# Pairs counted two in a number, and the attention layer's masks and words taken from other places

## The chip, the cores and the metric

The kernel runs on one core of one Trainium2 chip. The metric is the device time of one execution in microseconds (us), lower being better. Before the change it is 4636.71 us, the median of three runs (4636.35 to 4637.34).

## The reference

A graph of N = 3125 nodes with 256 features each and E = 50,000 edges, sorted by destination, goes through four graph layers, with a residual and a layer normalization around each:

```python
edge_index = jnp.stack([src, dst])
x = _layernorm(x + _L0_gnn_ref(x, edge_index, W, b))            # degree-normalized sum over edges, then @ W
x = _layernorm(x + _L1_gnn_ref(x, src, dst, ...))               # attention over each node's edges, 8 heads of 32
x = _layernorm(x + _L2_gnn_ref(x, edge_index, ...))             # attention, then three mean-aggregation layers
x = _layernorm(x + _L3_gnn_ref(x, weight, edge_weight1, src, dst, edge_type_16))   # 16 relations
```

Of the first layer, what the change concerns is how often each pair (destination, source) occurs and how many edges begin and end at each node. Of the second:

```python
e = leaky_relu(el[src] + er[dst], 0.2);  m = segment_max(e, dst);  e = exp(e - m[dst])
a = e / segment_sum(e, dst)[dst];        out = segment_sum(feat[src] * a[:, :, None], dst)
```

## The kernel before

Nodes lie in T = 25 tiles of 128. Edges lie in S = 416 slots of 128, each slot belonging to one tile of destinations; `words_i` has one number for every four slots, which says where among them one tile ends and the next begins. Each function of the kernel is a block: the five engines run their own programs in it, order them by semaphores, and meet at its end.

**Counting pairs** (`count_pairs`, L479 to L634, called once). For each slot, VectorE (DVE) writes two one-hot matrices in bfloat16. `hot_d` (L536) is 128 edges x 128 destinations. `hot_s` is 128 edges x 3125 sources, in two instructions (L538: 1600 columns, L540: 1525), because a comparison number beyond 2048 isn't exact in float16. TensorE (PE) multiplies the two into `counts`, seven PSUM banks of up to 512 columns (`product`, L560), which collect over all slots of a tile. A 3126th column of ones gives the edges per destination. Where a tile ends inside a group of four slots, PE closes the banks (L557), ScalarE (ACT) copies each to `rows` (L621), and SyncE stores the 128 x 3200 numbers to `pairs_d` (L630); PE's next product into a bank waits for its copy. `marked` and `hist` (L525, L527, L576) count the edges per source in the same loop, once for four slots. `hot_d` and `hot_s` have four buffers, handed back by `used`. PE alone reads `words_i` (`load_word`, L81), by a load into a register of its sequencer.

**The attention layer** (`attend`, L1323 to L1694) walks the slots in 13 parts of 32. GpSimd (POOL) gathers a slot's 128 rows of `feat_d` with one indirect DMA (L1377) into `got`, which holds two parts. When a part has arrived, PE turns its scores (L1561). DVE and PE find the maximum per destination (`maximum`, from L1437 to L1488). PE deals the next scores out into `spreads` (`deal`, L1539). DVE then writes, for every four slots, the masks `hot` (L1498: `iota` compared with `dloc`) and the weighed rows (L1502), eight times in a part. PE multiplies them into `sums` (L1604) behind a matmul that restores the carried sums (L1599), and reads the part's eight words just ahead of it (`total`).

Of the kernel before, what the change touches and what calls it, by code (L numbers as in the profile page):

```python
# [478 lines left out]
def count_pairs(nc, k, pairs_d, links_d):  # L479
# [7 lines left out]
    with ExitStack() as c:  # L487
# [23 lines left out]
        @block.gpsimd  # L511
        def _(pool):
            pool.iota(places[:], [[1, HALF]], base=0, channel_multiplier=0,
                      allow_small_or_imprecise_dtypes=True).then_inc(ready, 1)
            pool.memset(zero[:], 0.0).then_inc(ready, 1)
            pool.memset(hot_s[:, :, N:N + 1], 1.0).then_inc(ready, 1)
            pool.memset(rows[:, :, N:NP], 0.0).then_inc(ready, 1)

        @block.vector
        def _(dve):  # L520
            dve.tensor_scalar(upper[:], k.src[:], float(-HALF), None, ALU.add).then_inc(ready, 1)
            dve.wait_ge(ready, 5)
# [7 lines left out]
            with dve.Fori(0, S // 8) as i:  # L530
                for u in range(8):
                    j = i * 8 + u
                    if u % 4 == 0:
                        marks(2 * i + u // 4, u // 4)
                    dve.wait_ge(used, j + 1)
                    dve.tensor_scalar(hot_d[:, u % 4, :], k.iota_b[:], cols(k.dloc, j, 1), None,  # L536
                                      ALU.is_equal).then_inc(made, 1)
                    dve.tensor_scalar(hot_s[:, u % 4, 0:HALF], places[:], cols(k.src, j, 1), None,  # L538
                                      ALU.is_equal).then_inc(made, 1)
                    dve.tensor_scalar(hot_s[:, u % 4, HALF:N], places[:, 0:N - HALF], cols(upper, j, 1), None,  # L540
                                      ALU.is_equal).then_inc(made, 1)
            dve.wait_ge(final, 1)
            dve.tensor_copy(k.deg_src[:], hist[:, 0:T])

        @block.tensor
        def _(pe):
            pe.sem_inc(used, 4)
            pe.sem_inc(tallied, 2)
            pe.wait_ge(ready, 5)

# [12 lines left out]
            def multiply(u, j):  # L563
                pe.wait_ge(made, j * 3 + 3)
# [14 lines left out]
            def four(i, b):  # L579
                tally(i, b)  # L580
                word = load_word(pe, k, i)
                with pe.If((word & 15) == 0):
                    for u in range(4):
                        multiply(u, i * 4 + u)
                with pe.If((word & 15) != 0):

                    for u in range(4):
                        with pe.If(turn_here(word, u) == 0):
                            multiply(u, i * 4 + u)
                        with pe.If(turn_here(word, u) != 0):  # L590
                            t = tile_before(word, u)
                            for b in range(BANKS):
                                end(b).then_inc(full, 1)
                            pe.wait_ge(made, (i * 4 + u) * 3 + 3)
                            for b in range(BANKS):

                                pe.wait_ge(copied, t * COPIES + COPIES + (b + 1 if b < BANKS - 1 else COPIES))
                                last = product(u, b, True)
                            last.then_inc(used, 1)
# [4 lines left out]
            pe.matmul(hist[:, 0:T], zero[0:EP, 0:P], zero[0:EP, 0:T], start=False, stop=True).then_inc(final, 1)  # L604
            for b in range(BANKS):
                end(b).then_inc(full, 1)

        @block.scalar
        def _(act):
            act.sem_inc(copied, COPIES)  # L610

            def copy(t, b):
                if reused(t):
                    act.wait_ge(stored[b], (t - b) * 8)
                act.sem_inc(k.passed, 1)
                for n in range(BANKS):
                    act.wait_ge(full, t * BANKS + n + 1)
                    act.sem_inc(k.passed, 1)
                    if n == BANKS - 1:
                        act.copy(cols(k.deg_dst, t, 1), counts[:, n, width[n]:width[n] + 1]).then_inc(copied, 1)  # L620
                    act.copy(rows[:, b, n * 512:n * 512 + width[n]], counts[:, n, 0:width[n]]).then_inc(copied, 1)  # L621
            over_tiles_after_two(act, copy)

        @block.sync
        def _(sp):
            sp.dma_start(links_d.rearrange("d (g q) p -> q d g p", q=SQ), k.links[:]).then_inc(linked, 16)

            def store(t, b):
                sp.wait_ge(copied, t * COPIES + 2 * COPIES)
                sp.dma_start(pairs_d[bass.ds(t * P, P), :], rows[:, b, :]).then_inc(stored[b], 16)  # L630
# [692 lines left out]
def attend(nc, k, table, links_d, er, acc, den):  # L1323
# [6 lines left out]
    with ExitStack() as c:  # L1330
# [62 lines left out]
        def _(dve):  # L1393
# [97 lines left out]
            def weigh(n):  # L1491
                b = n % 2
                dve.wait_ge(weights, 2 * n + 1)
                for g in range(NG):
                    if n >= 1:
                        dve.wait_ge(multiplied, (n - 1) * NG + g + 1)
                    j = n * CS + 4 * g
                    dve.tensor_tensor(hot[:, 4 * g:4 * g + 4, :], k.iota[:].unsqueeze(1).broadcast_to([P, 4, P]),  # L1498
                                      k.dloc[:, j:j + 4].unsqueeze(2).broadcast_to([P, 4, P]), ALU.is_equal).then_inc(made, 1)
# [3 lines left out]
                                      ALU.mult).then_inc(weighed, 1)  # L1503

            step(dve.memset(penx[:], -BIG))
            dve.sem_inc(cleared, 1)
# [25 lines left out]
        def _(pe):  # L1532
# [61 lines left out]

            def total(n, b, more):
                words = [load_word(pe, k, n * NG + g) for g in range(NG)]
                pe.wait_ge(resumed, n + 1)
# [35 lines left out]
            pe.wait_ge(er_kept, 1)  # L1633
            deal(0)
            pe.wait_ge(seamed, 1)
# [344 lines left out]
def graph_layers(nc, x, src, dst, edge_type_16, edge_weight1, L0_gnn_W, L0_gnn_b, L1_gnn_W_lin, L1_gnn_b_lin,  # L1980
# [12 lines left out]
    with ExitStack() as c:  # L1993
# [9 lines left out]
        k.zero = sb("zero", [P, T])  # L2003
        k.unordered = sb("unordered", [1, 1], I32)
        k.words_i = sb("words_i", [1, S // 4], I32)
        k.parts_i = sb("parts_i", [1, NC], I32)
# [10 lines left out]
        with ExitStack() as l:  # L2017
# [5 lines left out]
            order_edges(nc, k, [src, dst, edge_type_16, edge_weight1.rearrange("e a -> (e a)").bitcast(I32)], dst)  # L2023
            fill_slots(nc, k)
            count_pairs(nc, k, pairs_d, links_d)

# [226 lines left out]
```

## Time and profile before

| | us |
|---|---|
| median of three runs | 4636.71 |
| the profiled execution, whole | 4640.11 |
| its span in the profile | 4638.3 |
| PE, DVE, POOL, ACT busy | 3766.8, 1928.5, 1310.2, 578.0 |
| counting pairs, first mark to the next block | 83.0 to 756.2 |
| gathers of the attention layer, first to last | 1243.2 to 1813.9 |

The profile gives for each engine its busy time and what it waited for. A matmul in it is a weight load (PEld) and a product (PE). A granted clock of 1.00 is 2.4 GHz and 0.50 is 1.2 GHz. Names such as `c_`, `a_` and `t_` before a tile are those of the function: counting, attention, first layer.

### The profile page before, as it was taken

How to read it: one execution, taken by the hardware profiler on the slowest of the kernel's cores; microseconds unless marked ns; L12 is line 12 of the kernel's file. 1: busy time of each engine (PE TensorE's matmuls, PEld its weight loads, DVE VectorE, ACT ScalarE, POOL GpSimd, SP SyncE). 2: the span in 40 equal slices, each digit the busy share in tenths (PEclk: the TensorE clock that was granted, in tenths of full speed). 3: DMA queues.
4: the chain of work that ended last, by engine and by line, in shares of the span. 5: the costliest groups of instructions: out<-in, count | busy, mean ns of one | idle time of the engine just before them, and what ended most of it. 6: DMA issues, size and time to landing. Idle time of an engine off the chain costs nothing. (4 is left out here: it accounts for less than half of the span.)

```text
span 4638.3 us, 49117 instructions
## 1 busy us (share of the span) xinstructions
PE 3766.8 (81%) x14814; PEld 2235.0 (48%) x14871; DVE 1928.5 (42%) x4570; ACT 578.0 (12%) x1119; POOL 1310.2 (28%) x923
## 2 busy tenths in 40 slices
PE   3999988996646666379999979999999689965665
PEld 1444434564445454256666645655655434434444
DVE  6998884012467777633232201211122411132223
ACT  0001112222101001012222200000000012200000
POOL 1000000000277775027777600000000000047776
PEclk9999999998767777689999989999999899987787
DMA  1011125763244442011221143443433134433334
GB/s 49 14 42 58 83 99 189 234 217 129 93 120 124 116 126 64 12 74 61 76 75 62 61 160 117 136 136 116 138 134 116 49 131 145 145 119 105 104 105 120
DMA packets 240236, 493.51 MB, mean 106 GB/s; under 512 B 22617, under 2 KB 137853, under 8 KB 231885
## 3 DMA queue, kind: packets, MB, share of 16 engines
q1 hardware_dynamic: 199693, 380.62, 23.8%
q0 software_dynamic: 40448, 111.66, 8.6%
q8 instruction: 54, 0.88, 0.1%
q14 instruction: 41, 0.34, 0.0%
HBM read 347.63 MB, written 145.38 MB: 106 GB/s over the span
## 5 line engine op out<-in xcount | busy, mean ns | idle before, releaser
L1257 POOL DMA_INDIRECT e7got<-rel_d,rel_i x416 | 394.9, 949 | 1551.3 <-POOLq L2138 1424.8
L1377 POOL DMA_INDIRECT a_got<-feat_d,src_i x416 | 445.2, 1070 | 1287.0 <-POOLq L1703 1160.6
L560 PE MATMUL c_counts<-c_hot_s,c_hot_d 128*128 128x512 bf16 (+1 forms) x2857 | 603.0, 357 | 49.6 <-ACT c_rows L621 18.2
L946 PE MATMUL s_aggs<-s_blk,h 128*128 128x512 f32 (+1 forms) x1400 | 549.6, 549 | 17.9 <-DMA s_blk<-turned_d 17.9
L1293 PE MATMUL e7sums<-e7got,e7hot 128*128 128x256 f32 x832 | 289.7, 508 | 194.1 <-DMA e7got<-rel_d,rel_i 164.9
L560 PEld LDWEIGHTS c_counts<-c_hot_s,c_hot_d 128*128 128x128 bf16 x2912 | 258.7, 98 | 366.6 <-ACT c_rows L621 66.1
L946 PEld LDWEIGHTS s_aggs<-s_blk,h 128*128 128x128 f32 x1400 | 264.2, 191 | 268.6 <-issue 176.2
L2179 PE MATMUL q_prods<-w,q_xt 128*128 128x512 f32 x800 | 352.8, 599 | 13.4 <-ACT q_xt L2197 13.4
L1038 DVE TENSOR_SCALAR s_zs<-s_prods,col 128x256 f32<-128x256 f32 x75 | 36.3, 484 | 751.7 <-PE s_prods L972 751.7
L1293 PEld LDWEIGHTS e7sums<-e7got,e7hot 128*128 128x128 f32 x832 | 204.5, 256 | 276.4 <-issue 238.0
L1109 POOL TENSOR_SCALAR g_absent<-g_pairs 128x3200 bf16<-128x3200 f32 x25 | 274.8, 10992 | 169.4 <-DMA g_pairs<-pairs_d 169.3
L1156 PE MATMUL g_sums<-value,g_turned 128*128 128x257 f32 x1250 | 299.1, 383 | 8.6 <-ACT g_turned L1220 8.6
L1134 PE MATMUL g_scores<-key_t,g_q 128*128 128x512 f32 (+1 forms) x700 | 278.3, 554 | 27.4 <-DMA g_q<-query_d 20.3
L811 PE MATMUL t_aggs<-t_blk,r 128*128 128x512 f32 (+1 forms) x700 | 299.5, 550 | 0.0
L946 PE MATMUL s_aggs<-s_blk,spare 128*128 128x512 f32 (+1 forms) x700 | 273.8, 547 | 0.0
L1265 DVE TENSOR_SCALAR e7hot<-iota,dloc,weight 128x128 f32<-128x128 f32 x416 | 115.8, 364 | 356.7 <-PE e7sums L1293 348.2
L538 DVE TENSOR_SCALAR c_hot_s<-c_places,src 128x1600 bf16<-128x1600 f16 x416 | 261.9, 630 | 0.0
L540 DVE TENSOR_SCALAR c_hot_s<-c_places,c_upper 128x1525 bf16<-128x1525 f16 x416 | 255.8, 615 | 0.0
L2179 PEld LDWEIGHTS q_prods<-w,q_xt 128*128 128x128 f32 x800 | 151.0, 191 | 200.6 <-issue 199.9
L1156 PEld LDWEIGHTS g_sums<-value,g_turned 128*128 128x128 f32 x1250 | 226.4, 191 | 43.1 <-issue 7.6
L1604 PE MATMUL a_sums<-a_got,a_hot 128*128 128x264 f32 x832 | 234.3, 444 | 0.2
L1134 PEld LDWEIGHTS g_scores<-key_t,g_q 128*128 128x128 f32 x700 | 130.0, 192 | 176.8 <-issue 142.0
(365 smaller groups left out, 4056.9 us busy)
## 6 DMA issues: line engine op xcount, KB each, us to landing
s_blk<-turned_d SPq DMA_DIRECT2D x60, 1280.0 KB, 5.7
rel_d<-q_rows SPq DMA_DIRECT2D x25, 2048.0 KB, 7.5
s_blk<-turned_d SPq DMA_DIRECT2D x45, 960.0 KB, 4.9
pairs_d<-c_rows SPq DMA_DIRECT2D x25, 1600.0 KB, 5.2
g_pairs<-pairs_d SPq DMA_DIRECT2D x25, 1600.0 KB, 6.6
t_blk<-pairs_d SPq DMA_DIRECT2D x20, 1280.0 KB, 7.1
turned_d<-t_line SPq DMA_DIRECT2D x20, 1280.0 KB, 9.7
t_blk<-pairs_d SPq DMA_DIRECT2D x15, 960.0 KB, 6.1
```

The lines of the kernel that those rows point to most:

```text
L538: dve.tensor_scalar(hot_s[:, u % 4, 0:HALF], places[:], cols(k.src, j, 1), None, ALU.is_equal).then_inc(made, 1)
L540: dve.tensor_scalar(hot_s[:, u % 4, HALF:N], places[:, 0:N - HALF], cols(upper, j, 1), None, ALU.is_equal).then_inc(made, 1)
L560: return pe.matmul(counts[:, b, 0:taken[b]], hot_d[:, u, :], hot_s[:, u, b * 512:b * 512 + taken[b]], start=first, stop=False)
L811: last = pe.matmul(aggs[:, n % 2, half, 0:w], r[:, a, half * P:(half + 1) * P], blk[:, q % RINGS, a % GA, 0:w], start=a == 0, stop=a == T - 1)
L946: last = pe.matmul(aggs[:, idx % 2, half, 0:w], feats[l][:, a, half * P:(half + 1) * P], blk[:, q % RINGS, a % GA, 0:w], start=a == 0, sto ...
L1109: pool.tensor_scalar(absent[:, b, :], pairs[:, b, :], 0.0, -BIG, ALU.is_equal, ALU.mult).then_inc(flagged, 1)
L1134: last = pe.matmul(scores[:, n % BUFS, 0:width[n]], q[:, b, a, :], key_t[:, a, n * 512:n * 512 + width[n]], start=a == 0, stop=a == 1)
L1156: last = pe.matmul(sums[:, b, 0:D + 1], turned[:, g % BUFS, a % 4, :], value[:, a, :], start=a == 0, stop=a == T - 1)
L1257: pool.indirect_dma_start(got[:, j % U, :], None, table, bass.IndirectOffsetOnAxis(ap=index[:, j:j + 1], axis=0)).then_inc(arrived[j % U / ...
L1293: return pe.matmul(sums[:, 0:D], hot[:, u, :], got[:, u, :], start=False, stop=False)
L1377: pool.indirect_dma_start(got[:, n % 2, s, :], None, table, bass.IndirectOffsetOnAxis(ap=k.src_i[:, j:j + 1], axis=0)).then_inc(arrived[n ...
L2179: last = pe.matmul(prods[:, o % 4, :], xt[:, b, a, :], w[:, a, 2 * o:2 * o + 2, :].rearrange("p r n -> p (r n)"), start=a == 0, stop=a == 1)
```

## The change

**Counting pairs.** A new block, `count_packed`, does the work of `count_pairs` with one column for two sources: source s and source s + 1563 share column s. A low source adds 1 to its column and a high one 4096, so a number in PSUM holds two counts of up to 4095. `hot_s` is one instruction of 1563 columns, which compares and multiplies by two per-partition numbers; a slot's product takes four banks (512, 512, 512 and 28 columns) in place of seven. `hot_d` and `hot_s` have eight buffers. When a tile closes, ACT copies the banks to `whole` as integers; DVE, two groups later, takes the low 12 bits and the high ones (`take_apart`); ACT copies both to `rows`, as float. To know that a tile has closed, DVE now reads the word of the group two back, in every group of four slots. The old block stays behind the new one, and each engine skips it unless `heavy`, computed at the new block's end, says that some node has more than 4095 edges.

```diff
+def count_packed(nc, k, pairs_d, links_d):
+    HALF = (N + 1) // 2
+    W = HALF + 1
+    LOOK = 2
+    RING = 4 * LOOK
...
+            step(dve.tensor_scalar(high[:], k.src[:], float(HALF), None, ALU.is_ge))
+            step(dve.scalar_tensor_tensor(column[:], high[:], float(-HALF), k.src[:], ALU.mult, ALU.add))
+            step(dve.tensor_scalar(value[:], high[:], 4095.0, 1.0, ALU.mult, ALU.add))
...
+            def take_apart(t):
+                dve.wait_ge(copied, t * COPIES + 2 * COPIES)
+                dve.wait_ge(spread_out, t * 2 + 2)
+                dve.tensor_single_scalar(apart[:, 0, :], whole[:], 4095, ALU.bitwise_and).then_inc(parted, 1)
+                dve.tensor_single_scalar(apart[:, 1, :], whole[:], 12, ALU.arith_shift_right).then_inc(parted, 1)
+
+            def closings(group):
+                word = load_word(dve, k, group)
+                with dve.If((word & 15) != 0):
+                    for u in range(4):
+                        with dve.If(turn_here(word, u) != 0):
+                            take_apart(tile_before(word, u))
...
-                    dve.tensor_scalar(hot_s[:, u % 4, 0:HALF], places[:], cols(k.src, j, 1), None,
-                                      ALU.is_equal).then_inc(made, 1)
-                    dve.tensor_scalar(hot_s[:, u % 4, HALF:N], places[:, 0:N - HALF], cols(upper, j, 1), None,
-                                      ALU.is_equal).then_inc(made, 1)
+                    dve.tensor_scalar(hot_s[:, u, 0:HALF], places[:, 0:HALF], cols(column, j, 1), cols(value, j, 1),
+                                      ALU.is_equal, ALU.mult).then_inc(made, 1)
...
+                    act.copy(whole[:, n * 512:n * 512 + here], counts[:, n, 0:here]).then_inc(copied, 1)
...
+                for half in range(2):
+                    act.wait_ge(parted, t * 2 + half + 3)
+                    act.copy(rows[:, b, half * HALF:(half + 1) * HALF], apart[:, half, :]).then_inc(spread_out, 1)
```

In the counting loop, DVE's program for one slot was (the ISA and ALU rows are its sequencer's)

```order
L535 REGISTER_ALU
L536 ISA
L536 TENSOR_SCALAR c_hot_d<-iota_b,dloc 128x128
L538 REGISTER_ALU
L538 TENSOR_SCALAR c_hot_s<-c_places,src 128x1600
L540 REGISTER_ALU
L540 TENSOR_SCALAR c_hot_s<-c_places,c_upper 128x1525
```

and is now

```order
L726 REGISTER_ALU
L727 ISA
L727 TENSOR_SCALAR u_hot_d<-iota_b,dloc 128x128
L728 ISA
L728 TENSOR_SCALAR u_hot_s<-u_places,u_column,u_value 128x1563
```

Ahead of each group of four slots its program now has (L81 is the word, L714 the test whether a tile closes in the group, L716 the same for one slot, L705 and L707 the waits of `take_apart`)

```order
L81 TENSOR_LOAD words_i
L81 ISA x2
L714 REGISTER_ALU
L714 COMPARE_AND_BRANCH
L716 REGISTER_ALU
L716 COMPARE_AND_BRANCH
L705 ISA
L707 ISA
L709 TENSOR_SCALAR u_apart<-u_whole 128x1563
L710 TENSOR_SCALAR u_apart<-u_whole 128x1563
```

A slot went from three instructions to two, and a load with a test came in front of each group.

**The attention layer.** The masks' `iota` is copied once into PSUM, to the free columns of `spreads`, and L1498 reads it there; since `deal` writes the same bank, DVE waits before a part's masks until the deal issued just before them has ended. PE's eight words of a part are loaded at its start, ahead of `maximum`.

```diff
                 dve.wait_ge(weights, 2 * n + 1)
+                dve.wait_ge(dealt, min(n + 3, NC + 1))
...
-                    dve.tensor_tensor(hot[:, 4 * g:4 * g + 4, :], k.iota[:].unsqueeze(1).broadcast_to([P, 4, P]),
+                    dve.tensor_tensor(hot[:, 4 * g:4 * g + 4, :], spreads[:, 256:256 + P].unsqueeze(1).broadcast_to([P, 4, P]),
...
             def chunk(n, b, more):
+                words = [load_word(pe, k, n * NG + g) for g in range(NG)]
                 maximum(n, b, more)
-                total(n, b, more)
+                total(n, b, more, words)
```

PE's program around the end of a part's maxima was

```order
L1552 MATMUL a_expand<-a_er,a_pick 128x24 x8
L1539 ISA
L1539 MATMUL a_spreads<-tile_hot,a_er_rows 128x32 x8
L81 ISA
L81 TENSOR_LOAD words_i
L81 ISA x3
```

with seven more such loads before `L1599 MATMUL a_sums<-a_carry,ident`; now the deal is followed directly by the restoring matmul:

```order
L1764 MATMUL a_expand<-a_er,a_pick 128x24 x8
L1751 ISA
L1751 MATMUL a_spreads<-tile_hot,a_er_rows 128x32 x8
L1810 MATMUL a_sums<-a_carry,ident 128x264
```

The eight loads stand at the loop's head instead, ahead of the part's first `a_expand` and of the turned lines (`a_line`) that DVE's maxima wait for.

## Rows read from the trace of the kernel before

**Rows 1.** The profile's page: busy us (share of the span) xinstructions

```profile
PE 3766.8 (81%) x14814; PEld 2235.0 (48%) x14871; DVE 1928.5 (42%) x4570; ACT 578.0 (12%) x1119; POOL 1310.2 (28%) x923
```

**Rows 2.** Waits between 60 and 800 us: total us, times, longest

```profile
DVE c_hot_d L536 <- PE c_counts L560: 53.6, 53, 2.2
```

**Rows 3.** Timeline of the counting, one group: start, us, engine, instruction

```profile
401.06 0.68 DVE L525 TENSOR_TENSOR c_marked<-iota_b,slo 125x512 bf16<-125x512 bf16 x1
...
401.83 0.24 DVE L536 TENSOR_SCALAR c_hot_d<-iota_b,dloc 128x128 bf16<-128x128 bf16 x1
401.99 0.62 DVE L538 TENSOR_SCALAR c_hot_s<-c_places,src 128x1600 bf16<-128x1600 f16 x1
402.54 0.61 DVE L540 TENSOR_SCALAR c_hot_s<-c_places,c_upper 128x1525 bf16<-128x1525 f16 x1
403.07 0.24 DVE L536 TENSOR_SCALAR c_hot_d<-iota_b,dloc 128x128 bf16<-128x128 bf16 x1
...
406.77 0.68 DVE L525 TENSOR_TENSOR c_marked<-iota_b,slo 125x512 bf16<-125x512 bf16 x1
```

**Rows 4.** Stretches: us, busy of PE PEld DVE ACT POOL, clock, DMA, GB/s

```profile
90.00:150.00 60.00, 56.84 (x331) 26.75 (x334) 59.71 (x147) 0.00 (x0) 0.00 (x0) 1.00 0.00 1
1500.00:1600.00 100.00, 60.09 (x305) 47.15 (x303) 73.08 (x122) 8.21 (x17) 77.76 (x74) 0.73 0.45 130
```

**Rows 5.** Timeline of PE's weight loads after a tile's end

```profile
207.61 0.15 PEld L560 LDWEIGHTS c_counts<-c_hot_s,c_hot_d 128*128 128x128 bf16 x1 [0.28 <-issue]
208.04 0.15 PEld L560 LDWEIGHTS c_counts<-c_hot_s,c_hot_d 128*128 128x128 bf16 x1 [0.28 <-issue]
...
210.35 0.18 PEld L576 LDWEIGHTS c_hist<-c_marked 125*128 125x128 bf16 x4
...
215.79 0.18 PEld L576 LDWEIGHTS c_hist<-c_marked 125*128 125x128 bf16 x4
```

**Rows 6.** DVE's timeline: one per-partition number, then two

```profile
759.45 6.66 DVE L875 TENSOR_SCALAR r<-X,col 128x256 f32<-128x256 f32 x25
...
4628.58 1.38 DVE L1908 TENSOR_SCALAR acc<-acc,mv,rstd 128x256 f32<-128x256 f32 x4
```

**Rows 7.** DVE's groups, busy us, mean ns: integers; an odd number of columns

```profile
L200 DVE TENSOR_SCALAR p_bits<-p_sn 125x400 int32<-125x400 int32 x1 | 0.4, 369 | 3.4 <-DMA p_nxt<-in_dst 3.4
L238 DVE TENSOR_SCALAR p_cmpj<-p_ioj,p_ends 25x417 f32<-25x417 f32 x1 | 0.4, 425 | 0.0
```

**Rows 8.** A part's word loads, 1510 to 1531 us: ns min/median/max, first to last

```profile
L81 PEldq TENSOR_LOAD <-words_i x8: 297/298/309, 1524.8 to 1530.1; - x8
```

**Rows 9.** An ACT group over SBUF: busy us, mean ns

```profile
L1213 ACT ACTIVATE g_probs<-g_probs,g_top 128x3200 f32<-128x3200 f32 x25 | 74.1, 2964 | 26.4 <-DVEq L1188 26.4
```

**Rows 10.** SyncE's timeline, the first load of the block after the counting

```profile
756.23 6.84 SPq L778 DMA_DIRECT2D t_blk<-pairs_d  x5
```

**Rows 11.** DVE's register load ahead of a block that it skips

```profile
L349 DVEq TENSOR_LOAD <-unordered x1: 546/546/546, 38.9 to 38.9; - x1
```

**Rows 12.** The gathers, and DVE's first scan of a part: ns, first and last start

```profile
L1377 POOL DMA_INDIRECT a_got<-feat_d,src_i x416: 942/946/1823, 1243.2 to 1813.9; - x139
...
L1437 DVE TENSOR_TENSOR_SCAN a_turned<-a_penx,a_turned x13: 2282/2283/2283, 1288.6 to 1819.8; 32x1024 f32<-32x1024 bf16 x13
```

**Rows 13.** Waits between 1155 and 1890 us

```profile
DVE a_turned L1437 <- PE a_turned L1561: 108.5, 13, 24.2
```

**Rows 14.** Timeline of the attention layer: the deal, the masks, the gathers

```profile
1524.66 3.62 PE L1539 MATMUL a_spreads<-tile_hot,a_er_rows 25*128 x16
...
1527.26 0.69 DVE L1498 TENSOR_TENSOR a_hot<-iota,dloc 128x512 f32<-128x512 f32 x1 [0.22 <-DVE a_carry L1488]
...
1529.00 0.68 DVE L1498 TENSOR_TENSOR a_hot<-iota,dloc 128x512 f32<-128x512 f32 x1
1529.08 1.43 POOL L1377 DMA_INDIRECT a_got<-feat_d,src_i  x1 [0.30 <-issue]
1529.60 1.21 DVE L1502 TENSOR_TENSOR a_got<-a_got,a_peaks 128x1024 f32<-128x1024 f32 x1
```

**Rows 15.** DVE's groups: one input in PSUM, both in SBUF

```profile
L1041 DVE TENSOR_TENSOR s_zs<-s_zs,be 128x256 f32<-128x256 f32 x75 | 31.9, 425 | 2.6
L1039 DVE TENSOR_TENSOR s_zs<-s_zs,s_prods 128x256 f32<-128x256 f32 x75 | 31.6, 421 | 2.6
```

More of the change, by code:

```diff
@@ new lines, in _, with copy @@
+        @block.scalar
+        def _(act):
+            heavy = act.value_load(k.heavy[:], min_val=0, max_val=1)
+            with act.If(heavy != 0):
+                act.sem_inc(copied, COPIES)
+                def copy(t, b):
+                    if reused(t):
+                        act.wait_ge(stored[b], (t - b) * 8)
+                    act.sem_inc(k.passed, 1)
+                    for n in range(BANKS):
+                        act.wait_ge(full, t * BANKS + n + 1)
+                        act.sem_inc(k.passed, 1)
+                        if n == BANKS - 1:
+                            act.copy(cols(k.deg_dst, t, 1), counts[:, n, width[n]:width[n] + 1]).then_inc(copied, 1)
+                        act.copy(rows[:, b, n * 512:n * 512 + width[n]], counts[:, n, 0:width[n]]).then_inc(copied, 1)
+                over_tiles_after_two(act, copy)
@@ new lines, in _, with store @@
+        @block.sync
+        def _(sp):
+            heavy = sp.value_load(k.heavy[:], min_val=0, max_val=1)
+            with sp.If(heavy != 0):
+                sp.dma_start(links_d.rearrange("d (g q) p -> q d g p", q=SQ), k.links[:]).then_inc(linked, 16)
+                def store(t, b):
+                    sp.wait_ge(copied, t * COPIES + 2 * COPIES)
+                    sp.dma_start(pairs_d[bass.ds(t * P, P), :], rows[:, b, :]).then_inc(stored[b], 16)
+                over_tiles(sp, store)
+                sp.wait_ge(linked, 16)
+                sp.wait_ge(stored[0], 16 * (T // 2 + 1))
+                sp.wait_ge(stored[1], 16 * (T // 2))
@@ new lines, in count_packed, with _ @@
+def count_packed(nc, k, pairs_d, links_d):
+    HALF = (N + 1) // 2
+    W = HALF + 1
+    BANKS = -(-W // 512)
+    COPIES = BANKS + 1
+    LOOK = 2
+    RING = 4 * LOOK
+    with ExitStack() as c:
+        c.enter_context(nc.cleanup_on_exit())
+        sb = lambda n, s, d=F32: c.enter_context(nc.sbuf_tensor("u_" + n, s, d))
+        sem = lambda n: nc.alloc_semaphore("u_" + n)
+        places = sb("places", [P, HALF + 1], F16)
+        high, column, value = sb("high", [P, S]), sb("column", [P, S]), sb("value", [P, S])
+        hot_d = sb("hot_d", [P, RING, P], BF16)
+        hot_s = sb("hot_s", [P, RING, W], BF16)
+        zero = sb("zero", [P, 512], BF16)
+        whole = sb("whole", [P, HALF], I32)
+        apart = sb("apart", [P, 2, HALF], I32)
+        rows = sb("rows", [P, 2, NP])
+        largest, flag = sb("largest", [P, 1]), sb("flag", [1, 1])
+        marked = sb("marked", [EP, 2, 4, P + T], BF16)
+        hist = c.enter_context(nc.psum_tensor("u_hist", [P, 512], F32))
+        counts = c.enter_context(nc.psum_tensor("u_counts", [P, BANKS, 512], F32))
+        (ready, made, used, hot, tallied, final, full, copied, parted, spread_out, linked, vstep) = (sem(n) for n in (
+            "ready", "made", "used", "hot", "tallied", "final", "full", "copied", "parted", "spread_out", "linked", "vstep"))
+        reduced, laid = sem("reduced"), sem("laid")
+        stored = [sem(f"stored{b}") for b in range(2)]
+        taken = [min(512, W - b * 512) for b in range(BANKS)]
+        block = c.enter_context(nc.Block())
+        @block.gpsimd
+        def _(pool):
+            pool.iota(places[:], [[1, HALF + 1]], base=0, channel_multiplier=0,
@@ L563, in multiply @@
             def multiply(u, j):
[L564 removed]
+                pe.wait_ge(made, j * 2 + 2)
                 for b in range(BANKS):
```

169 lines of the change are left out of this document (139 added, 30 removed).

## The prediction

> **What bounds the kernel now.** I read the page first: PE is busy for most of the span, DVE for under half [rows 1]. Such shares mix stages, so I took the two stages of the change apart, by stretches, waits and timelines.
>
> In the counting, DVE is busy 59.71 of 60 us before the first tile closes, and PE 56.84 [rows 4]. The timeline shows why: a group of four slots takes DVE 5.71 us, mark to mark, 0.77 for the marks and 1.24 for each slot, which is 0.16 (`hot_d`), 0.55 and 0.53 (`hot_s`) from start to start [rows 3]. PE, where it is behind and has not to wait, does a group in 5.44 us [rows 5]. So DVE sets the pace and PE is close behind. DVE's own waits for PE, 53.6 us, come where tiles close and four buffers don't bridge the copies [rows 2].
>
> In the attention layer the waits name the other end. DVE stands 108.5 us for a part's turned scores, 24.2 of it for the first part [rows 13], and these wait for the gathers. A part takes (1819.8 - 1288.6) / 12 = 44.3 us [rows 12]; DVE waits (108.5 - 24.2) / 12 = 7.0 of it, so its own chain is 37.3. POOL's gathers set the pace: one every 1.375 us ((1813.9 - 1243.2) / 415), though one takes 0.946 [rows 12] and 0.30 to issue [rows 14].
>
> **Counting: the masks.** The two `hot_s` instructions become one of 1563 columns. 1600 columns cost 0.55 us and 1525 cost 0.53 [rows 3]; 75 columns for 0.02 us fits four a cycle at 0.96 GHz, also for the odd 1525, and leaves 0.13 us fixed. So 1563 columns are 0.54 us. The second per-partition number costs extra: with one, (6.66 - 0.35) / 24 = 0.263 us from start to start, with two (1.38 - 0.41) / 3 = 0.323, both for 256 float columns [rows 6]. I add 0.06: 0.60 for `hot_s`, 0.76 for a slot, 0.77 + 4 x 0.76 = 3.81 for a group, 396 us for 104 groups. No row shows two per-partition numbers in bfloat16. The bounds are four columns a cycle and one: 0.60 and 1563 / 0.96 + 0.19 = 1.82 us. I take the first, since in floats the two-number form keeps the pace of the one-number form but for the 0.06.
>
> **Counting: taking apart.** 25 tiles bring two integer instructions each. 400 integers took 0.369 us and an odd 417 floats 0.425 [rows 7], less than 417 / 0.96 = 0.434: two a cycle. 1563 / 1.92 + 0.13 = 0.94 us, 50 of them 47 us; at one a cycle it would be 88.
>
> **Counting: words and tests on DVE.** 104 loads and tests. On PE's sequencer a load takes 0.30 us and one follows another after 0.76 [rows 8]; with the test about 0.85. If DVE's sequencer is far enough ahead of its engine, this costs nothing; if not at all, 88 us. In front of a group the queued `hot_s` covers 0.6, and eight buffers let DVE's sequencer run ahead. I take 0.1 each, 10 us.
>
> **Counting: what is late next.** A group of PE's has 12 full matmuls fewer. One is 0.213 us at 2.4 GHz, so 5.44 - 12 x 0.213 = 2.88, under DVE's 3.81; PE waits for DVE throughout. At a closing, PE's four banks come back behind ACT's copies at 0.5 us steps, some 2 us, less than the 3 us of four more slots made. ACT adds two copies of 1563 numbers, 1.45 us each by its 2.96 us for 3200 [rows 9]; with the banks about 5 us of the 9 that even the shortest tile lasts. DVE's `take_apart` waits for copies made two groups before. I allow 20 us for closings in which one waits for the other, against 53.6 now. The loop becomes 396 + 47 + 10 + 20 = 473 us. It was 741.6 - 83.0 = 658.6, that is 104 x 5.71 = 594 and the waits. Gain 185.
>
> **Around the loop.** From DVE's last mask to the next block's first load it was 741.6 to 756.2 [rows 10]. Now PE is less far behind (3 us), three banks fewer are copied (1 us), but 0.94 + 2 x 1.45 us of taking apart come before the last store: no change. The old block is skipped: one register load of 0.55 us [rows 11], a jump over long code and one more meeting of the engines. The trace shows no long jump; 1 to 6 us, I take 3.
>
> **Attention: masks from PSUM.** A gather that starts under a mask (1529.08, mask from 1529.00) takes 1.43 us in place of 0.95, while the weighing (L1502), which has one input in PSUM, lengthens none [rows 14]. A mask and a weighing together last 1.73 us, exactly gather plus issue, so the two lock together, seven or eight times in a part: 7.5 x 0.48 = 3.6 us. That fits the 32 x (1.375 - 1.246) = 4.1 by which a part's gathers are over their undisturbed pace. So the gathers would allow 40.7 us for a part. The read from PSUM itself costs nothing by the one pair that compares it: 421 ns with an input in PSUM, 425 without [rows 15].
>
> Two rules of the Trainium skill speak against this edit. The page "VectorE: DVE Perf Modes", section "The TRN2 errata", gives an instruction with a PSUM source 62 cycles more than one with SBUF sources. By that, as an estimate, 104 masks would lose 7 us, and the time be 4424; the rows just named disagree with it. The page "SBUF — State Buffer", section "Who interferes with whom", says that a `tensor_tensor` with both inputs in SBUF contends only with GpSimd's reads, and infers that it doesn't stall the generation of descriptors. By that a gather would not be longer under a mask and the edit would gain nothing (4455); the 1.43 us row contradicts it here.
>
> **Attention: the wait and the words.** The masks now wait for `deal`. It ends at 1524.66 + 3.62 = 1528.28, and the first mask starts at 1527.26 [rows 14]: 1.0 us later, and behind it stand all weighings, PE's products and the next part's scores. The eight words take 8 x 0.76 = 6.1 us of PE's sequencer [rows 8]. Until now they delayed PE behind the deal, where DVE wasn't waiting. At the head they run while PE's engine still works off the last part's products, but what isn't finished delays the turned lines that DVE's maxima need: 0 to 6.1 us, I take 1.5, because some 4.5 us of queued products stand in front. DVE's chain becomes 37.3 + 1.0 + 1.5 = 39.8 us, just under the gathers' 40.7. So a part gains up to 3.6 us, 12 parts 43; as the two ends are so close I take 38.
>
> **Sum.** The profiled execution took 4640.1 us (span 4638.3 and 1.8 around it): 4640.1 - 185 + 3 - 38 = 4420. It was 3.4 us above the median of the three runs, so I predict 4417.
>
> **Rivals.**
> 1. *The attention layer gives nothing.* The words at the head delay DVE by their whole 6.1 us: 37.3 + 1.0 + 6.1 = 44.4, the part's period of now. For it: DVE waits for these very lines soon after PE's last products. Against it: those products are queued ahead. 4417 + 38 = 4455. Chance 0.16.
> 2. *DVE pays for control and integers in full.* 78 us more for the words, 41 for one integer a cycle; 10 more at the arms: 4546. Against it: rows 7, and the deeper buffers. 0.10 for this or most of it.
> 3. *TensorE drops to 1.2 GHz and becomes the bound.* In the counting the clock is 1.00 with PE busy 95%, in the attention layer 0.73 with 60% [rows 4]; the new counting would be near 75%. After a closing's wait, loads follow at 0.43 us [rows 5], which is 1.2 GHz. Held there, a group costs PE 12 x 0.43 + 0.35 = 5.5 us, 104 of them 573, with closings 615, not 473: 4559. Against it: it would then be busy without gaps, and that is where these rows show the full clock. 0.06.
> 4. *The double mask doesn't run four columns a cycle.* At two, a slot is 1.17 us and the loop 654: 4598, chance 0.03. At one, a slot is 1.98 us, a group 8.7, the loop 904 + 47 + 20 = 971: 4417 + 498 = 4915, slower than before. This is the case on the other side; it decides once `hot_s` costs more than about 1.15 us, where the loop passes 658.6 + 35. It has no row against it in the same types, only the float rows. 0.04.
>
> **Chances.** The forecast has 0.61, with 4380 to 4450 for itself: the loop between 443 and 493 us, the attention layer between 43 and 25. Range 4375 to 4500: it holds rival 1 and half of rival 2, and leaves out the other half, rival 3 and rival 4. A change under 0.2% can't be told from none here. Faster 0.94 (all but rival 4 at one column, and mixes of its half pace with exposed words), same 0.01, slower 0.05.
>
> **What would show it.** Right: `hot_s` at about 0.68 us in the groups and 0.60 from start to start; `apart` at about 1.0 us; groups 3.8 to 4.0 us apart before the first tile closes; the loop over by 560 us. Gathers at 0.95 us under the masks, and first scans 41 us apart. Wrong: `hot_s` over 1 us; gaps of 0.5 us and more in front of the marks with DVE's sequencer loading a word; PE's matmuls at 0.43 us through the stage; DVE waiting for `turned` not at all in the attention layer, with 44 us between scans.

## The result, and the profile after

The changed kernel takes 4389.53 us (median of four runs, 4388.77 to 4392.23), the one before 4636.53 beside it (4634.40 to 4637.34). The ratio is 0.9469, with the 95% interval 0.9453 to 0.9485: faster by 247 us. The forecast was 4417, with 4375 to 4500 as range.

The page of the changed kernel answers to [rows 1]: span 4387.5 us, PE 273 us less busy, DVE 154.

```profile
PE 3493.4 (80%) x13533; PEld 2105.8 (48%) x13546; DVE 1774.5 (40%) x4212; ACT 612.8 (14%) x1094; POOL 1269.4 (29%) x923
```

**The counting.** A stretch before the first tile closes (us, busy of PE, PEld, DVE, ACT, POOL, clock, DMA, GB/s) answers to [rows 4]. DVE has no gap, and PE is now 81% busy in place of 95%, still at the full clock.

```profile
90.00:140.00 50.00, 40.42 (x274) 19.40 (x273) 50.00 (x132) 0.00 (x0) 0.00 (x0) 1.00 0.00 0
```

DVE's timeline (start, us, engine, instruction) shows a group, answering to [rows 3], and a closing behind the next one:

```profile
300.14 0.69 DVE L699 TENSOR_TENSOR u_marked<-iota_b,slo 125x512 bf16<-125x512 bf16 x1
...
300.91 0.25 DVE L727 TENSOR_SCALAR u_hot_d<-iota_b,dloc 128x128 bf16<-128x128 bf16 x1
301.08 0.69 DVE L728 TENSOR_SCALAR u_hot_s<-u_places,u_column,u_value 128x1563 bf16<-128x1563 f16 x1
301.67 0.25 DVE L727 TENSOR_SCALAR u_hot_d<-iota_b,dloc 128x128 bf16<-128x128 bf16 x1
...
303.95 0.69 DVE L699 TENSOR_TENSOR u_marked<-iota_b,slo 125x512 bf16<-125x512 bf16 x1
...
307.77 0.97 DVE L709 TENSOR_SCALAR u_apart<-u_whole 128x1563 int32<-128x1563 int32 x1
308.66 0.97 DVE L710 TENSOR_SCALAR u_apart<-u_whole 128x1563 int32<-128x1563 int32 x1
309.54 0.69 DVE L699 TENSOR_TENSOR u_marked<-iota_b,slo 125x512 bf16<-125x512 bf16 x1
```

Mark to mark is 303.95 - 300.14 = 3.81 us; a slot is 0.76 (300.91 to 301.67), of which `hot_s` has 0.60 from start to start. A closing (the two integer instructions that follow where a tile ended) costs 309.54 - 307.77 = 1.77. The marks at 303.95 start with no gap, though DVE's program has a word loaded and tested ahead of them. Over the whole loop the answer for DVE's line of `hot_s` (ns min/median/max, first and last start) and that of the integers, with what DVE waited for there, are

```profile
L728 DVE TENSOR_SCALAR u_hot_s<-u_places,u_column,u_value x416: 673/689/703, 84.4 to 520.7; 128x1563 bf16<-128x1563 f16 x139
```

```profile
L709 DVE TENSOR_SCALAR u_apart<-u_whole x25: 957/970/980, 167.4 to 527.1; 128x1563 int32<-128x1563 int32 x25
its engine sat idle before it (us, times) until:
  ACT u_whole L824: 4.0, 1
  issue: 0.2, 1
```

The 4.0 us are those of the last tile, behind the loop. Inside it DVE waits for nobody; the wait of [rows 2] is gone, and PE waits for DVE instead (total us, times, longest):

```profile
PE u_counts L761 <- DVE u_hot_d L727: 42.3, 50, 1.9
```

The loop, first mark to where DVE's last `hot_s` gives way to the next instruction, is 521.3 - 83.5 = 437.8 us against 658.6: 221 us less. What follows is longer. DVE's and SyncE's timeline from the loop's end to the next block, for [rows 10]:

```profile
520.71 0.69 DVE L728 TENSOR_SCALAR u_hot_s<-u_places,u_column,u_value 128x1563 bf16<-128x1563 f16 x1
...
527.15 0.97 DVE L709 TENSOR_SCALAR u_apart<-u_whole 128x1563 int32<-128x1563 int32 x1 [3.99 <-ACT u_whole L824]
...
530.22 0.14 DVE L744 CAST heavy<-u_flag 1x1 int32<-1x1 f32 x1
542.21 7.07 SPq L988 DMA_DIRECT2D t_blk<-pairs_d  x5
```

That is 20.9 us where it was 14.6. The next block starts 756.23 - 542.21 = 214.0 us earlier.

**The attention layer.** Its first gather starts 213.9 us earlier. The gathers and DVE's first scan of each part, for [rows 12]:

```profile
L1587 POOL DMA_INDIRECT a_got<-feat_d,src_i x416: 942/946/1851, 1029.3 to 1559.4; - x139
```

```profile
L1647 DVE TENSOR_TENSOR_SCAN a_turned<-a_penx,a_turned x13: 2282/2283/2283, 1074.4 to 1568.8; 32x1024 f32<-32x1024 bf16 x13
```

A part takes (1568.8 - 1074.4) / 12 = 41.2 us in place of 44.3, and the gathers take 530.1 us from first to last in place of 570.7. The last scan is 37 us nearer to the first gather (539.5 in place of 576.6), the last mask 34 (572.9 in place of 606.5). The masks of before and of after, in the same columns:

```profile
L1498 DVE TENSOR_TENSOR a_hot<-iota,dloc x104: 679/683/693, 1305.8 to 1849.7; 128x512 f32<-128x512 f32 x104
```

```profile
L1709 DVE TENSOR_TENSOR a_hot<-a_spreads,dloc x104: 680/681/692, 1093.0 to 1602.2; 128x512 f32<-128x512 f32 x104
```

DVE's waits there, for [rows 13]:

```profile
DVE a_turned L1647 <- PE a_turned L1773: 41.5, 9, 24.3
DVE a_hot L1709 <- PE a_spreads L1751: 15.1, 12, 1.6
DVE a_lines L1658 <- PE a_small L1782: 13.1, 9, 5.9
```

Besides the old wait for the turned scores there are two new ones: the masks for the deal, 1.3 us a part, and the lines, for which PE is late because of its words. The timeline of a part's masks answers to [rows 14]:

```profile
1298.99 0.69 DVE L1709 TENSOR_TENSOR a_hot<-a_spreads,dloc 128x512 f32<-128x512 f32 x1 [1.34 <-PE a_spreads L1751]
...
1300.11 0.94 POOL L1587 DMA_INDIRECT a_got<-feat_d,src_i  x1 [0.30 <-issue]
1300.72 0.68 DVE L1709 TENSOR_TENSOR a_hot<-a_spreads,dloc 128x512 f32<-128x512 f32 x1
1301.32 1.21 DVE L1713 TENSOR_TENSOR a_got<-a_got,a_peaks 128x1024 f32<-128x1024 f32 x1
1301.35 0.94 POOL L1587 DMA_INDIRECT a_got<-feat_d,src_i  x1 [0.30 <-issue]
...
1302.45 0.68 DVE L1709 TENSOR_TENSOR a_hot<-a_spreads,dloc 128x512 f32<-128x512 f32 x1
1302.60 0.95 POOL L1587 DMA_INDIRECT a_got<-feat_d,src_i  x1 [0.31 <-issue]
```

The gather of 1302.60 starts 0.15 us into a mask and takes 0.95 us. (The one of 1300.11 is no test: it is there before its mask, and such gathers weren't lengthened in the kernel before either.) Counted over both traces: in the kernel before, 95 gathers start while a mask runs; those that start 0.07 us into it take 1.43 us, those 0.45 us into it 1.06. In the 12 during which a mask starts, none takes over 0.95. In the changed kernel 56 start while a mask runs and 71 have one start during them, and none takes over 0.96.

214.0 and 33.6 us make 247.6; the spans differ by 250.8. The other 3 lie in the layers behind, which the change doesn't touch.

### The profile page after: what moved, and what is told of

The parts are those of the page before. It is cut to its first block and busy times, and to the rows that moved or that the text cites. A ratio compares the mean times of both kernels' runs of the same rounds, so it can differ in the third digit from the quotient of the medians.

```text
span 4387.5 us, 46641 instructions
## 1 busy us (share of the span) xinstructions
PE 3493.4 (80%) x13533; PEld 2105.8 (48%) x13546; DVE 1774.5 (40%) x4212; ACT 612.8 (14%) x1094; POOL 1269.4 (29%) x923
## 5 line engine op out<-in xcount | busy, mean ns | idle before, releaser
L1587 POOL DMA_INDIRECT a_got<-feat_d,src_i x416 | 404.6, 973 | 1072.6 <-POOLq L1916 946.3
L761 PE MATMUL u_counts<-u_hot_s,u_hot_d 128*128 128x512 bf16 (+1 forms) x1653 | 328.6, 341 | 90.5 <-DVE u_hot_d L727 42.3
L728 DVE TENSOR_SCALAR u_hot_s<-u_places,u_column,u_value 128x1563 bf16<-128x1563 f16 x416 | 286.6, 689 | 0.0
L761 PEld LDWEIGHTS u_counts<-u_hot_s,u_hot_d 128*128 128x128 bf16 x1664 | 136.6, 99 | 256.9 <-DVE u_hot_d L727 53.1
L1815 PEld LDWEIGHTS a_sums<-a_got,a_hot 128*128 128x128 f32 x832 | 177.2, 221 | 64.1 <-issue 28.7
```

The source lines that it names most:

```text
L728: dve.tensor_scalar(hot_s[:, u, 0:HALF], places[:, 0:HALF], cols(column, j, 1), cols(value, j, 1), ALU.is_equal, ALU.mult).then_inc(made, 1)
L761: return pe.matmul(counts[:, b, 0:taken[b]], hot_d[:, u, :], hot_s[:, u, b * 512:b * 512 + taken[b]], start=first, stop=False)
L1587: pool.indirect_dma_start(got[:, n % 2, s, :], None, table, bass.IndirectOffsetOnAxis(ap=k.src_i[:, j:j + 1], axis=0)).then_inc(arrived[n ...
L1815: ins = pe.matmul(sums[:, 0:W], hot[:, 4 * g + u, :], got[:, b, 4 * g + u, :], start=False, stop=False)
```

## The experiments

Two questions were open: how much each part of the change gives, and why the counting loop was 35 us shorter than I had worked out. The first four kernels ran on one chip with the kernel before (4637.52 us, seven runs).

**c_only.** `count_packed` as changed, `attend` as before.

> The counting part of the change alone, the attention layer as before. Theory (the two parts are independent; the counting gave 214 us of the 247 and the attention layer 37, as the two profiles read side by side): 4636.5 - 214 = about 4423 us, and the gathers 1.375 us apart again. Rival (the counting gave the 182 us that the prediction gave it, and the rest comes from the two parts together): about 4455 us.

Measured: 4425.52 us (4422.67 to 4427.52), ratio 0.9543 [0.9527, 0.9559]. So the counting gives 212 us; the trace of the changed kernel had said 214. Its gathers (busy us, mean ns, then idle time) are still long, 1069 ns in the mean:

```profile
L1587 POOL DMA_INDIRECT a_got<-feat_d,src_i x416 | 444.5, 1069 | 1073.0 <-POOLq L1913 946.6 <-issue 125.8 <-PE a_sums L1814 0.6
```

**a_only.** `attend` as changed, counting as before.

> The attention layer's part alone, the counting as before. Theory: 4636.5 - 37 = about 4600 us, a part's first scans 41.2 us apart. Rival (the attention layer gains only behind the shorter counting): 4636 us.

Measured: 4608.26 us (4607.73 to 4608.45), 0.9937 [0.9920, 0.9953]: 29 us less, 8 short of what I expected. After c_only's 4425.5, the attention part is worth 36. Inside the layer both do the same: 529.8 us of gathers (mean 972 ns), 572.9 to the last mask, 33.6 less than before. The difference of 7 isn't in the layer. Between the profiled executions it is 3: with the new counting the span is 34.7 us shorter (32.1 of it in the layer), with the old one 31.9 (33.6 in the layer).

**a_masks_old.** The changed kernel with the masks reading `iota` in SBUF and no wait for the deal; the words stay at the head.

```diff
-                dve.wait_ge(dealt, min(n + 3, NC + 1))
...
-                    dve.tensor_tensor(hot[...], spreads[:, 256:256 + P].unsqueeze(1).broadcast_to([P, 4, P]),
+                    dve.tensor_tensor(hot[...], k.iota[:].unsqueeze(1).broadcast_to([P, 4, P]),
```

> The changed kernel with the masks read from SBUF again and without their wait for the deal; the words stay at the part's head. Theory: the gathers take 1.43 us under a mask again, first scans 44.3 us apart, 4389.5 + 37 = about 4427 us. Rival (the words bring at least half of the gain): 4408 us or less.

Measured: 4430.20 us (4428.65 to 4431.02), 0.9553 [0.9537, 0.9569]; gathers 1031.8 to 1600.0, the old pace. The words alone gain nothing; against c_only they cost some 5 us, and they cost them at the end: from the last scan to the last mask it is 35.2 us here and 29.4 in c_only.

**a_words_old.** The changed kernel with the words behind the deal.

```diff
-                words = [load_word(pe, k, n * NG + g) for g in range(NG)]
                 maximum(n, b, more)
-                total(n, b, more, words)
+                total(n, b, more)        # which loads the words itself, at its start
```

> The changed kernel with TensorE's eight words loaded where they were, behind the deal; the masks still read PSUM and wait for the deal. Theory (the masks alone bring the attention layer's gain, and the words at the head only delay the turned lines, by 16.9 us in ten parts): DVE waits for the lines no more, first scans 40.9 us apart in place of 41.2, about 4386 us, no slower than 4390. Rival (the words' new place is what lets TensorE follow, so without it each part is 2.6 us longer): about 4420 us.

Measured: 4380.11 us (4379.57 to 4382.99), 0.9445 [0.9429, 0.9460], 9 us under the changed kernel. That one was measured in another series, and the two intervals just touch, so the 9 us rest on the traces below and on the last run of this section as well. So the masks from PSUM gave 45 us against c_only, and the words at the head took back 9. The gathers of this kernel,

```profile
L1587 POOL DMA_INDIRECT a_got<-feat_d,src_i x416 | 404.3, 972 | 1074.7 <-POOLq L1916 948.2 <-issue 124.9 <-PE a_sums L1816 1.5
```

are those of the changed one (mean 973), from the first to the last 529.8 us against 530.1. So the middle parts gain nothing from either place of the words. By the traces the 9 us lie where no gather is left to issue. PE's timeline in the last part, changed kernel first:

```profile
1567.62 1.04 PE L1773 MATMUL a_turned<-ident,a_got 128*32 128x128 f32 x8
...
1573.16 0.28 PE L1805 MATMUL a_sums<-zero_b 128*128 128x264 bf16 x1
1578.11 0.37 PE L1782 MATMUL a_small<-ident,a_line 32*8 32x32 f32 x4 [4.68 <-issue]
```

```profile
1565.19 1.03 PE L1773 MATMUL a_turned<-ident,a_got 128*32 128x128 f32 x8 [0.41 <-DMA a_got<-feat_d,src_i]
...
1571.55 0.27 PE L1782 MATMUL a_small<-ident,a_line 32*8 32x32 f32 x4 [0.55 <-DVEq L1652]
```

The last gathers start at 1559.4 and 1561.3. With the words behind the deal PE waits for that gather's rows and turns them 3.9 us after it was issued; with the words ahead it is still busy with products that its late start had pushed back, and turns them 8.3 us after. Then PE's engine stands 4.68 us with nothing but the sequencer's loads between two matmuls, and DVE stands 3.8 us for the lines. The last scan starts 9.4 us after the last gather in one kernel and 5.1 in the other: 4.3 + 3.8 = 8.1 us, of the 9.4 between the medians.

**c_ring4 and c_words3.** Four buffers for `hot_d` and `hot_s` in place of eight; and each word of DVE loaded three times. The next four kernels ran on a chip where the kernel before took 4936.52 us. Their gathers take 754 to 767 us from first to last, against 530, though each instruction still takes 0.97 in the mean; so only what lies inside the counting loop is compared with the runs above. DVE's instructions there have the same length (`hot_s` 685 ns).

```diff
-    RING = 4 * LOOK
+    RING = 4          # and every buffer index u taken mod 4
```
```diff
                 word = load_word(dve, k, group)
+                word = load_word(dve, k, group)
+                word = load_word(dve, k, group)
```

> The changed kernel with four buffers for the counting's masks in place of eight. Theory (eight buffers are what took DVE's waits for TensorE, 53.6 us, away and let its sequencer hide the words): DVE waits at each of 24 closings some 1 to 2 us and in some groups for the word: 4389.5 + 40 = about 4430. Rival (with four banks in place of seven TensorE is so far ahead that four buffers would do): 4395 or less.

Measured: 4836.56 us, 0.9796 [0.9750, 0.9843]. The loop is 84 us longer, twice what I expected:

```profile
L728 DVE TENSOR_SCALAR u_hot_s<-u_places,u_column,u_value x416: 679/685/699, 84.6 to 605.4; 128x1563 bf16<-128x1563 f16 x139
```

Its waits of DVE in the loop:

```profile
DVE u_apart L709 <- issue: 40.5, 23, 2.4
DVE u_hot_d L727 <- PE u_counts L761: 31.0, 48, 2.0
DVE u_marked L699 <- issue: 4.5, 9, 0.7
```

31 us are the old wait for PE at closings, which eight buffers cover. 40.5 us stand in front of the 23 closings in the loop with nothing named but issue: there, as I read it, DVE's sequencer had stood with its engine for a buffer, and so was not ahead when the closing's tests came. The 31 us are to be held against the 53.6 of [rows 2], with four buffers and seven banks.

> The changed kernel with DVE loading each word three times. Two more loads are 1.5 us of its sequencer per group, 2.4 us with the first, against 3.8 us of its engine. Theory (the sequencer runs ahead of the engine by the depth of its queue, and a load costs nothing while it does): the queue covers one load but not three, the groups grow by some 0 to 1 us: 4390 to 4490, middle 4420. Rival (loads never show while the sequencer's sum is under the engine's 3.8 us): 4390, no change. Second rival (a load that is not covered by chance costs all of its 0.76): 4389.5 + 104 x 1.5 = 4546.

Measured: 4806.55 us, 0.9740 [0.9694, 0.9785]. The loop is 576.5 - 83.5 = 493.0 us between first and last `hot_s`, 56.7 longer (inside what I expected), for 208 loads more: 0.27 us each. Its waits in the loop:

```profile
DVE u_apart L709 <- issue: 31.9, 23, 2.3
DVE u_marked L699 <- issue: 16.5, 34, 0.8
```

Even with three loads only 34 marks of 103 stand, half a microsecond each; most of the cost is at the closings, as in c_ring4. There too the marks hardly stand (4.5 us), so a group's single load and test are nearly hidden with four buffers as well. What four buffers lose would then be the work queued on DVE when a closing's tests and branches come; no run separates the two.

**a_bank and a_spread.** The masks' numbers in a free quarter of the bank of `expand`, so that the masks wait for this part's expansion and not for the deal; and besides, the words loaded two and six at a time between the quarters of the scores.

```diff
-                dve.wait_ge(dealt, min(n + 3, NC + 1))
+                dve.wait_ge(expanded, min(n + 2, NC))
...
-                    ... spreads[:, 256:256 + P] ...
+                    ... expand[:, 0, 384:384 + P] ...
```

> The changed kernel with the masks' numbers kept in the free columns of another PSUM bank (expand), which TensorE has written for the last time of a part before its deal; the masks wait for that. The words stay at the head. Theory (the wait for the deal, 15.1 us in 12 parts, is on DVE's chain, and DVE's chain is what ends last in several parts): DVE is 1.3 us per part earlier, up to 9 us less, 4381 to 4388. Rival (the gathers alone set the pace): 4389.5, no change.

> As the kernel with the masks in the other bank, and two of the eight words loaded behind the second quarter of the scores and six behind the third, where TensorE's sequencer waits for DVE anyway (1.6 and 4.9 us). Theory: neither the wait for the deal nor the lines delay DVE, the gathers set the pace in all 12 parts: first scans 40.8 us apart, 4389.5 - 12 x 0.4 = 4385, or, counting what the words' return to their old place gave, 4375 to 4380. Rival (six words take 4.6 us of the 4.9 and delay the peaks): 4385 or more.

Measured: 4728.60 us and 4730.36, 0.9576 [0.9531, 0.9620] and 0.9578 [0.9534, 0.9623]. On that chip the two can't be told from each other, and the slow gathers cover what they could have shown: inconclusive. a_spread was run again, and a_bank in a variant with the words behind the deal, on a chip where the kernel before took 4639.51:

> As the run with the numbers in the expanded scores' bank, but the words are loaded inside the maxima's part on TensorE: two after the second quarter of the next part's scores, six after the third. If loading words costs only where DVE waits for TensorE, loads beside DVE's maxima are hidden, and the time is 0 to 10 us under the version with the words behind the deal. Rival: each quarter of scores is itself awaited by DVE, and the words delay it by up to 0.76 us each, 6 us a part at most: 5 to 20 us over it.

> The changed kernel with two edits of the attention layer. The numbers that the masks read lie in a free quarter of the bank of the expanded scores, so that the masks wait for this part's expansion and not for the deal of the part after the next; and TensorE loads a part's eight words behind the deal, as the kernel before did. If the deal wait (15.1 us over ten parts in the changed kernel) and the words at the head (9 us by the run that undid them alone) both lie on DVE's chain, the time is 9 + 10 to 15 us under the changed kernel: 4365 to 4371. Rival: with the deal wait gone DVE waits as much longer for the turned scores, and the time is the 4380 of the words alone. The last: masks that are made earlier collide with the gathers' issue, which takes the gain back (4385 to 4395).

Measured: a_spread2 (the same kernel as a_spread) 4387.31 us (4386.98 to 4388.68), 0.9454 [0.9441, 0.9467]; a_bank_words_old 4387.48 (4385.64 to 4389.98), 0.9453 [0.9440, 0.9465]. I expected 4365 to 4371 for the second and at most 4380 for the first: two misses. Of my rivals for the second, one foretold the waits and another the time. The wait for the deal is gone, and the wait for the gathers has grown by 12 us:

```profile
DVE a_turned L1647 <- PE a_turned L1773: 63.0, 12, 24.3
DVE a_turned L1670 <- PE a_small L1790: 8.4, 12, 0.9
```

50.8 us there in a_words_old became 63.0. DVE is ready earlier and stands longer, since the gathers set the pace. That rival gave 4380, though. The 4385 to 4395 that came were the third case's, by which earlier masks collide with the gathers; its mechanism isn't in the trace, where no gather under a mask takes over 0.96 us. What the trace has is 2.6 us more from first to last gather and 7.0 from the last gather to the last scan, against 5.1. The ratios' intervals of the two kernels overlap. For a_spread2 the rival's range (5 to 20 us over a_words_old) holds the time.

**c_noskip.** The changed kernel without the call of `count_pairs` behind the new block.

> The changed kernel without the block of the general pair count, which this input skips: DVE, ACT, POOL and SP no longer step over its instructions. My term for it was the distance from the last instruction of the counting loop on DVE to the next block, 20.9 us after against 14.6 before. If stepping over the longer block is what that distance consists of, the time falls by 4 to 12 us under the changed kernel's 4389.5 (4378 to 4386). If the distance is the last group's own chain (histogram, take-apart, copies on ACT) and the block's barrier, it falls by 0 to 3 us. Within these runs it also stands for the changed kernel beside the two attention variants.

Measured: 4391.77 us (4387.04 to 4397.87), 0.9467 [0.9454, 0.9480]. As a whole it can't be told from the changed kernel, so of my two cases it is the one of 0 to 3 us. In its trace the last instruction of the new block and the next block's first load stand closer:

```profile
530.55 0.14 DVE L744 CAST heavy<-u_flag 1x1 int32<-1x1 f32 x1
537.54 7.46 SPq L988 DMA_DIRECT2D t_blk<-pairs_d  x5
```

7.0 us in place of 12.0. The skipped block costs 5 us at its place; the first gather starts 4.3 us earlier, and 2.5 us are left in the span of the profiled execution.

**a_words_old_noskip.** Both together.

> The changed kernel with TensorE's eight words of a part behind the deal again, and without the block of the general pair count. My theory of the words at the head: while gathers are left to issue, their pace (1.25 us each) sets the attention layer and hides the words; in the last part nothing is left to issue, and there the words stand on the chain twice, 4.3 us ahead of the last scans and 3.8 us ahead of the lines after them. So the time from the last gather's start to the last scans falls from 9.4 to 5 us, the wait for the lines of that part from 3.8 to 0, the run's time by 8 us, and by 0 to 3 us more for the block: 4378 to 4382. Rival: the 9 us that the run with the words alone showed were spread over the parts or were scatter between runs, as the variant with the words behind the deal and the numbers in the other bank (4387) suggests: then 4386 to 4390.

Measured: 4378.42 us (4376.49 to 4382.33), 0.9442 [0.9429, 0.9455], before 4638.89. Gathers 1025.9 to 1556.1, last scan 1561.2: 5.1 us, and no wait for the lines, inside the 4378 to 4382 expected. Its median is the lowest of all, 11 us under the changed kernel, but it can't be told from a_words_old. It has no way to count a graph in which some node has over 4095 edges; a_words_old has.

## Why the prediction came out as it did

**The mechanism was right.** DVE is the counting's bound before and after, PE waits for it, and the gathers are the attention layer's.

**The masks: right.** Predicted `hot_s` 0.60 us, slot 0.76, group 3.81; measured the same three numbers. The second per-partition number costs as little in bfloat16 as in the float rows, so rival 4, the only slower case, was wrong in its condition. (Its sum for two columns a cycle was off by 10 besides: 104 x 5.45 + 47 + 10 + 20 = 644, not 654.)

**Taking apart: right.** Predicted 0.94 us an instruction and 47 us; measured 0.97 and 1.77 a closing. Only 23 of the 25 closings lie in the loop, 41 us; the last two come behind it, the first of them at 521.30.

**Words and closings: mis-sized.** These were my 10 and 20 us. 104 x 3.81 + 41 = 437.2, and the loop is 437.8: both terms together are under 1 us. The step that was mis-sized is above all "I allow 20 us for closings in which one waits for the other". With the 6 us of the last two tiles' integers the two terms are the whole 35 us by which the loop was shorter, and they put it below the 443 to 493 that the forecast had for it. c_ring4 shows where both went: take four buffers away and 31 us of waits for PE and 45 of issue come back. I had reckoned with the buffers for the words, and for the closings compared 2 us with 3 without drawing the conclusion, which is no wait at all. Rival 2 (words in full) has c_words3 against it.

**TensorE's clock: right in what mattered.** The granted clock was 1.00 before the first closing and 0.97, 0.94 and 0.93 in the stretches 140 to 300, 300 to 450 and 450 to 520 us; PE never became the bound. Rival 3 did not come.

**Around the loop: too low by 3 us.** Predicted 3, measured 6.3. Stepping over the old block is 5 of them by c_noskip, inside my 1 to 6; the rest, 1.3 us, would be the last tile's chain, which I had put at no change.

**The attention layer: predicted 38, measured 34.** That a gather is lengthened by a mask with both inputs in SBUF, and not by one with an input in PSUM, is shown: with SBUF masks the mean gather is 1070, 1069 and 1064 ns (before, c_only, a_masks_old), with PSUM masks 973, 972 and 972 (after, a_words_old, a_only). 416 x 0.097 = 40 us, which is the gathers' 570.7 - 530.1. The collisions were counted rightly: 95 in 13 parts, 7.3 a part for the 7.5 of the prediction. Nor is it the later start of the masks that keeps them apart: without the wait for the deal (a_bank_words_old and a_spread2, 978 and 982 ns) the gathers under masks take at most 0.96 us too. The Trainium skill, page "SBUF — State Buffer", section "Who interferes with whom", infers that a `tensor_tensor` doesn't stall the generation of descriptors; a gather's instruction is stalled by one here, so the forecast that the prediction drew from it (4455) is wrong. Whether it is the generation that stands or a read of SBUF by the same instruction, no run shows. The mask itself takes 681 ns against 683, so the 62 cycles of the Trainium skill's page "VectorE: DVE Perf Modes", section "The TRN2 errata", aren't to be seen here either. DVE's chain came out at 41.2 less (41.5 - 24.3) / 12 of waiting, 39.8 us, as predicted; but 37.3 + 1.0 + 1.5 rests on a guess for the words, so that the figure agrees is in part luck. What they cost I had put inside the part, and there they cost nothing; by the traces they cost 8 to 9 us once, in the last part. Without them the gain to the last mask is 42 us (1595.8 - 1031.5 = 564.3 in a_words_old), and 45 between the medians. Rival 1 took the words at their full 6.1 us in every part; the lines' waits reach 5.9 us, yet the gathers cover them.

**Sum.** 4420.1 for the profiled execution; -35.8 for the loop, +0.5 for its later start, +3.3 around it, +4.4 in the attention layer, and -3.2 in the layers behind: 4389.3, which is what the profiled execution took. The forecast was right as a time, and its largest error, the loop, is in one direction; the others took back 5 us of it.

What stays open: the 3 us of the layers behind, and why the attention part is worth 36 us behind the new counting and 29 behind the old; and whether a_spread2 and a_bank_words_old, whose gathers take 3 to 4 us longer from first to last than a_words_old's, are truly slower than it, which also leaves it open whether the words behind the deal are always worth their 9 us.

## What to carry to other kernels

A stage that is bound by one engine's chain, with its partner's stalls bridged by enough buffers, can be summed from start-to-start times, as here to 1 us in 438; compare each stall with the work buffered, and where it is shorter, write 0. With half the buffers the same loop took 84 us more. When a second resource sets the pace of a pipelined loop, look at the last round, where that resource has no more work: what was hidden in every round is paid there once. Where GpSimd issues gathers beside VectorE's masks, count the gathers that start while a mask runs. If the gathers set the pace, one input of the mask in PSUM can give that time back; read the mean gather before and after.

## What the runs showed of the hardware

- A gather's instruction on GpSimd that started 0.07 us into a VectorE `tensor_tensor` with both inputs in SBUF took 1.43 us, 0.45 us into it 1.06, and at most 0.95 when it had started first. With one input of the `tensor_tensor` in PSUM it took at most 0.96 either way; the mean of all gathers was 973 against 1070 ns.
- A `tensor_scalar` with two per-partition numbers, float16 in and bfloat16 out, ran 1563 columns in 0.60 us from start to start.
- DVE's sequencer hid one register load, a test and a branch in every 3.81 us. With four buffers in place of eight, DVE stood 1.8 us (40.5 / 23) in front of a closing; that its sequencer had been held by a buffer is how I read it.
- Eight loads on PE's sequencer left PE's engine idle for 4.68 us between two matmuls.
- On one of the chips the kernel before took 6% longer and a_spread 8% (4730 us, against 4387 for the same kernel elsewhere), with 754 us from first to last gather in place of 534 and an unchanged counting loop (436 and 437 us).
